# Two attention layers over eight images on one core: first query/key half moved to the last logits step, image 0's start reordered

## The chip, the cores and the metric

The kernel runs on one core of a Trainium2 chip. The metric is the device time of one launch in microseconds (us), lower is better. Five engines work side by side, each through its own instruction queue in order, and semaphores tie them together: TensorE (PE, matrix products into PSUM; PEld in the profile is its loading of weights), VectorE (DVE), ScalarE (ACT), GpSimd (POOL) and SyncE (SP, which here issues all transfers).

## The reference

For each of 8 images with 256 channels and 32x32 = 1024 pixels:

```python
# layer 0: self-attention with 32-channel query and key
q, k, v = Wq@x + bq, Wk@x + bk, Wv@x + bv          # 32, 32, 256 channels
x = gamma * (v @ softmax(q.T @ k).T) + x
# layer 1: group norm (32 groups), attention with 256-channel query and key
h = group_norm(x) * norm_w + norm_b
q, k, v = q_w@h + q_b, k_w@h + k_b, v_w@h + v_b
x = x + proj_w @ (v @ softmax(q.T @ k / 16).T) + proj_b
```

Everything is float32. The kernel splits a float32 operand into a rounded high part and a low remainder (`_hi`, `_lo`) and makes each product of three faster ones: high by high, high by low, low by high.

## The kernel before, in words

An image is 2 channel tiles of 128 by 1024 columns, in two halves of 512. Every 1024-column stage is cut into 8 tiles of 128 rows. Layer 0 of an image first makes `qk` (query and key projection, two entries, one for each half), `value0` (4 entries) and `scores` (8 tiles, only for the row maximum and the row sum of exponentials). From these comes a shift of each row, taken into the query operand by `shift`. `keys` (8 tiles) are the transposed scores with the shift, whose exponentials are the probabilities. `values(0, image, k)` multiplies value tile k by probability tile k and accumulates four PSUM banks over k (12 matmuls of 512 columns for each k). Layer 1 has `norm` (group sums), `query`, `value1`, `logits` (8 tiles, 12 matmuls each) and its own `values(1, ...)`.

PSUM is a `ring` of 4 slots of 1024 columns. Slots 2 and 3 hold the four accumulating banks of `values`; slots 0 and 1 pass all other results. An entry put into a slot waits until the reader of the entry before it there is done (`wait_read`, L583). A `scores` tile is read by DVE (row maximum, L1058) and then by ACT (exponential with row sum, L841); a `keys` tile by ACT (L817); a `qk` entry by ACT (L879, L884) and DVE (L1022, L1023, L1030). A probability tile goes through ACT (exponential, then the high part, L831 or L834) and DVE (the low part, L1075 or L1078), and only then may `values` use it.

The order is written out by hand as a list of `Step`s (L84 to L213). On TensorE (L777) a step fills its own `tile`, its `early` entries, the first `banks_first` banks of its `values`, its `sides`, the other banks, and its `late` entries. ACT and DVE walk over the same list in orders of their own (L906, L1135). `turn(i)` (L155) gives 16 steps: 0 to 7 make the keys of image i, 8 to 15 the logits of image i-1; `values` run two steps behind. In it `qk` of image i+1 has its first half late in step 0 and its second half in step 3, and `scores` of image i+1 begin in step 4. Image 1 has its turn written as `ones`; `turn` runs for images 2 to 7.

At the start (`first_image`, L84) TensorE is kept busy with products of ones (`keep_busy`, L590) while the first image is loaded in two halves of columns and split (L802, L955); then come `qk` and `value0` 0 and 1 of image 0, its 8 `scores` with `value0` 2 and 3 between them, `qk` of image 1, the shift (L635), and the keys steps. In the keys steps of image 0, step k+2 has `scores` k of image 1, always in slot 0.

Of the kernel before, what the change touches and what calls it, by code (L numbers as in the profile page):

```python
# [34 lines left out]
class Step:  # L35
# [6 lines left out]
    def __init__(self, tile=None, values=None, banks_first=2, slots=(0, 1)):  # L42
        self.tile, self.values, self.banks_first, self.slots = tile, values, banks_first, slots
        self.early, self.sides, self.late = [], [], []
        self.early_log = self.log = self.shifts = self.hidden = self.hidden_lo = self.split_x = self.x_lo_mid = self.x_lo_end = None
        self.statistics = self.evacuate = self.evacuate_at_once = None
        self.take_weights = self.keep_values = self.opening = self.rest = self.low_first = False
        self.early_in_front = False
        self.hidden_mid = None
# [34 lines left out]
def first_image():  # L84

    start, scores, opening = Step(slots=(0, 1, 2, 3)), Step(slots=(0, 1, 2)), Step()
    start.sides = tiles("qk", 0, (0, 1)) + tiles("value0", 0, (0, 1))
    scores.late = tiles("scores", 0, (0, 1, 2)) + tiles("value0", 0, (2,)) + tiles("scores", 0, (3, 4, 5))
    scores.late += tiles("value0", 0, (3,)) + tiles("scores", 0, (6, 7))
    scores.keep_values = True  # L90
# [7 lines left out]
    for k in range(6):  # L98
        steps[k + 2].early = tiles("scores", 1, (k,))
    steps[4].sides = tiles("value0", 1, (0,))  # L100
    steps[6].sides = tiles("value0", 1, (1,))
# [12 lines left out]
def second_image():  # L114
# [35 lines left out]
    ones[6].sides = tiles("shift", 2, (0,))  # L150
    ones[5].split_x, ones[5].x_lo_end, ones[6].x_lo_mid = 3, (3, 0), (3, 1)
    return steps + ones


def turn(i):  # L155
# [14 lines left out]
    if has(i + 1):  # L170
        steps[0].late = tiles("qk", i + 1, (0,))
        steps[3].banks_first = 0
# [21 lines left out]
    else:  # L194
# [3 lines left out]
        for m, s in enumerate((14, 15)):  # L198
            steps[s].late = tiles("query", i, (m,))
    if has(i + 2):  # L200
        steps[13].split_x, steps[13].x_lo_end, steps[14].x_lo_mid = i + 2, (i + 2, 0), (i + 2, 1)
    return steps
# [63 lines left out]
def values_done(tile):  # L266
# [12 lines left out]
    "v1_full", "v1_hi", "value1_split", "stats_ready", "norm_read", "coef_ready", "h_full", "h_hi", "h_split",  # L279
    "x_hi", "x_split", "res0_ready", "res1_ready", "weights_read", "weights_split", "rows_ready", "bias_read",  # L280
    "layer0_split", "v0_weights", "small_ready", "ones_ready", "key_hi", "link", "pool_link",
# [3 lines left out]
def build(nc, x, wqk_t, bqk, bk0, wv0_t, bv0, gamma, norm_w, norm_b, wq, bq, wk, bk, wv, bv, wp_t, bp,  # L285
          ident, group, y):
    with ExitStack() as ctx:
# [160 lines left out]
        def _(pool):  # L448
# [8 lines left out]
            def first_split_x():  # L457
                pool.wait_ge(x_loaded[1], x_loads(1))
                hi, lo = x_split(1)
                for half in range(HALVES):  # L460
                    cols = half_cols[half]
                    G.tensor_copy(hi[:, :, cols], x_in[1][:, :, cols]).then_inc(S["x_hi"], 1)
                    pool.wait_ge(S["x_hi"], 2 + half + 1)
                    G.tensor_tensor(lo[:, :, cols], x_in[1][:, :, cols], hi[:, :, cols].bitcast(F32),
# [112 lines left out]
        def _(pe):  # L577
# [139 lines left out]
            def fill(entry):  # L717
# [25 lines left out]
                else:  # L743
                    last = bias_products(SLOT[entry])
                last.then_inc(S["ring_ready"], 1)

            def values(tile, banks):
# [27 lines left out]
            wait("ones_ready", 1)  # L775
            keep_busy(ring[:, 3], 30)
            for now in STEPS:  # L777
                front = [now.tile] * bool(now.tile)
                for entry in now.early + front if now.early_in_front else front + now.early:
                    fill(entry)  # L780
                if now.values:
                    values(now.values, range(now.banks_first))
                for entry in now.sides:
                    fill(entry)
# [6 lines left out]
        def _(act):  # L791
# [3 lines left out]
            def split_x(i):  # L795
                for half in range(HALVES):
# [3 lines left out]
                    else:  # L800
                        act.wait_ge(x_loaded[i % 2], x_loads(i))
                    copy(x_hi[:, :, cols], x_in[i % 2][:, :, cols]).then_inc(S["x_hi"], 1)  # L802

# [49 lines left out]
            def project_hi(entry):  # L853
# [9 lines left out]
                if kind == "value0":  # L863
# [4 lines left out]
                    elif i:  # L868
                        copy(v0_hi[:, 2 * m:2 * m + 2], got).then_inc(S["value0_hi"], 1)
                if kind == "qk":  # L870
                    query_part(entry)
                    key_part(entry)

            def query_part(entry):
                _, i, m = entry
                if i == 0 and m == 0:
                    act.wait_ge(S["bqk_loaded"], 16 * 2)
                act.wait_ge(S["ring_ready"], RING_NO[entry] + 1)
                activation(q4[i % 2][0:64, half_cols[m]], half_place(entry)[0:64], ACT.Identity,  # L879
                           bias=bqk_s[0:64]).then_inc(S["qk_hi"], 1)  # L880

            def key_part(entry):
# [54 lines left out]
        def _(dve):  # L937
# [12 lines left out]
            scale = C ** -0.5  # L950

            def split_x(i, half):
                cols = half_cols[half]
                dve.wait_ge(S["x_hi"], 2 * i + half + 1)
                V.tensor_tensor(x_lo[:, :, cols], x_in[i % 2][:, :, cols], x_hi[:, :, cols].bitcast(F32),  # L955
# [10 lines left out]
            def first_weights():  # L966
                dve.wait_ge(S["wqk_loaded"], 16)
                split(wqk_hi[:], wqk_lo[:], wqk_f).then_inc(S["layer0_split"], 1)
                for half in range(HALVES):
                    split_x(0, half)  # L970

# [44 lines left out]
            def key_part(entry):  # L1016
# [4 lines left out]
                k, cols, out = k4[i % 2], half_cols[m], half_place(entry)  # L1021
                link(V.tensor_scalar(k[0:32, cols], out[64:96], bqk_s[64:96], None, ALU.add))  # L1022
                V.scalar_tensor_tensor(k[32:64, cols], out[64:96], bk0_s[:], k[0:32, cols].bitcast(F32),  # L1023
# [111 lines left out]
            for now in STEPS:  # L1135
# [28 lines left out]
                for entry in first:  # L1164
                    if entry[0] != "norm":
                        follow(entry)
# [9 lines left out]
                for entry in first:  # L1176
                    if entry[0] == "norm":
                        follow(entry)
# [48 lines left out]
```

## Time and profile before

| | |
|---|---|
| median of 3 runs | 795.13 us (795.07 to 798.98) |
| profiled execution | 795.73 us, its span 793.9 us |
| TensorE busy | 780.9 us, 98% |
| VectorE busy | 550.3 us, 69% |
| ScalarE busy | 468.8 us, 59% |
| GpSimd busy | 165.8 us, 21% |

The span is the time from the first to the last recorded instruction; the execution's own time is a little longer. Busy time is the sum of an engine's instructions, and says nothing yet of who waited for whom. "idle before, releaser" in a row of instructions is how long the engine stood idle in front of it and whose end let it go.

### The profile page before, as it was taken

To read this page: it belongs to the slowest core of one execution; us is meant where nothing else is said; L and a number is where in the kernel's file an instruction comes from. 1 tells how busy PE (TensorE), PEld (TensorE's weight loads), DVE (VectorE), ACT (ScalarE), POOL (GpSimd) and SP (SyncE) were. 2 spreads that over 40 slices of the span, in tenths; PEclk is the share of its full clock that TensorE was granted. 3 is DMA by queue.
4 is the path that set the end of the run, shared out by engine and by line. 5 is a ranking of instruction groups with operands and counts; after the bars stand their busy time and mean duration, and the time that the engine had idled before them with its cause. 6 is when DMAs were issued, how large, how long until landed. Compare 5 with 4: busy or idle time off the path is not lost.

```text
span 793.9 us, 9812 instructions
## 1 busy us (share of the span) xinstructions
PE 780.9 (98%) x3816; PEld 645.5 (81%) x3816; DVE 550.3 (69%) x790; ACT 468.8 (59%) x603; POOL 165.8 (21%) x147
## 2 busy tenths in 40 slices
PE   9899999999999999999999999999999999999998
PEld 8677888887888878887788877888778888888886
DVE  5866867777578765787657885577856756486564
ACT  4876656667555764567655586456864556445343
POOL 5640052013100231004210141102310024101120
PEclk9999999999999999999999999999999999999999
DMA  6010010002000110001100011000100001000101
GB/s 186 0 54 1 1 53 1 1 16 92 1 1 1 54 53 1 1 1 53 54 1 1 1 53 54 2 0 1 54 1 1 0 1 54 1 0 1 54 1 53
DMA packets 10366, 18.98 MB, mean 24 GB/s; under 512 B 2129, under 2 KB 3921, under 8 KB 10321
## 3 DMA queue, kind: packets, MB, share of 16 engines
q1 hardware_dynamic: 10320, 18.36, 6.7%
q8 instruction: 30, 0.49, 0.3%
q14 instruction: 16, 0.12, 0.1%
HBM read 9.97 MB, written 8.39 MB: 23 GB/s over the span
## 4 chain that ended last, share of the span: by engine, by line
PE 85%; DVE 9%; ACT 4%; issue 1%; POOL 0%; ACTq 0%; DVEq 0%; POOLq 0%
PE ring L596 26%; PE ring L598 25%; PE ring L597 25%; PE ring L606 4%; PE ring L616 3%; DVE res L1111 2%; DVE pt_lo L1075 2%; DVE h_lo L963 1%; ACT ring L841 1%; DVE q L1030 1%; PE ring L593 1%; DVE k L1022 1%; ACT pt_hi L831 1%; DVE k L1023 1%; ACT prob L817 1%
## 5 line engine op out<-in xcount | busy, mean ns | idle before, releaser
L596 PE MATMUL ring<-pt_hi,v_hi 128*128 128x512 f32 x480 | 189.1, 394 | 0.1
L598 PE MATMUL ring<-pt_hi,v_lo 128*128 128x512 f32 x480 | 187.9, 391 | 0.0
L597 PE MATMUL ring<-pt_lo,v_hi 128*128 128x512 f32 x480 | 187.7, 391 | 0.0
L820 ACT ACTIVATE prob<-ring,neg_max 128x1024 f32<-128x1024 f32 x64 | 71.6, 1119 | 156.6 <-DVE neg_max L1061 156.6
L1060 DVE TENSOR_REDUCE neg_raw<-ring 128x1 f32<-128x1024 f32 x64 | 78.2, 1223 | 59.0 <-PE ring L598 58.9
L503 POOL TENSOR_TENSOR v_lo<-v_f,v_hi 128x512 fp32r<-128x512 f32 x28 | 37.8, 1349 | 384.6 <-ACT v_hi L858 384.6
L598 PEld LDWEIGHTS ring<-pt_hi,v_lo 128*128 128x128 f32 x480 | 90.1, 188 | 19.8
L596 PEld LDWEIGHTS ring<-pt_hi,v_hi 128*128 128x128 f32 x480 | 90.2, 188 | 19.1 <-issue 1.7
L597 PEld LDWEIGHTS ring<-pt_lo,v_hi 128*128 128x128 f32 x480 | 90.3, 188 | 17.6
L1058 DVE TENSOR_REDUCE neg_max<-ring 128x1 f32<-128x1024 f32 x64 | 77.7, 1222 | 37.4 <-PE ring L606 37.3
L1075 DVE TENSOR_TENSOR pt_lo<-prob,pt_hi 128x1024 fp32r<-128x1024 f32 x64 | 81.6, 1276 | 30.4 <-ACT pt_hi L831 30.2
L841 ACT ACTIVATE ring<-ring,neg_max 128x1024 f32<-128x1024 f32 x64 | 69.6, 1087 | 43.4 <-DVE neg_max L1058 43.2
L1078 DVE SCALAR_TENSOR_TENSOR pt_lo<-prob,row_inv,pt_hi 128x1024 fp32r<-128x1024 f32 x64 | 83.1, 1298 | 15.0 <-ACT pt_hi L834 15.0
L596 PE MATMUL ring<-h_hi,query_hi 128*128 128x512 f32 x224 | 88.1, 393 | 0.2 <-DVE query_lo L1005 0.2
L598 PE MATMUL ring<-h_hi,query_lo 128*128 128x512 f32 x224 | 87.5, 391 | 0.0
L597 PE MATMUL ring<-h_lo,query_hi 128*128 128x512 f32 x224 | 87.5, 391 | 0.0
L817 ACT ACTIVATE prob<-ring 128x1024 f32<-128x1024 f32 x64 | 65.4, 1022 | 35.4 <-PE ring L616 35.1
L834 ACT ACTIVATE pt_hi<-prob,row_inv 128x1024 fp32r<-128x1024 f32 x64 | 73.9, 1154 | 11.0 <-DVE row_inv L1067 10.8
L831 ACT CAST pt_hi<-prob 128x1024 fp32r<-128x1024 f32 x64 | 67.4, 1054 | 5.3
L596 PEld LDWEIGHTS ring<-h_hi,query_hi 128*128 128x128 f32 x224 | 42.1, 188 | 9.3 <-DVE query_lo L1005 0.4
L598 PEld LDWEIGHTS ring<-h_hi,query_lo 128*128 128x128 f32 x224 | 42.0, 188 | 9.0
L597 PEld LDWEIGHTS ring<-h_lo,query_hi 128*128 128x128 f32 x224 | 42.1, 188 | 8.6
(167 smaller groups left out, 1347.1 us busy)
## 6 DMA issues: line engine op xcount, KB each, us to landing
out_y<-res SPq DMA_DIRECT2D x32, 256.0 KB, 2.2
x_in<-in_x SPq DMA_DIRECT2D x7, 1024.0 KB, 4.9
x_in<-in_x SPq DMA_DIRECT2D x2, 512.0 KB, 5.7
h_f<-in_wv_t SPq DMA_DIRECT2D x1, 256.0 KB, 4.0
res<-in_wq SPq DMA_DIRECT2D x1, 256.0 KB, 6.9
res<-in_wk SPq DMA_DIRECT2D x1, 256.0 KB, 7.2
res<-in_wv SPq DMA_DIRECT2D x1, 256.0 KB, 7.7
res<-in_wp_t SPq DMA_DIRECT2D x1, 256.0 KB, 7.4
```

The costliest lines, as they stand in the source:

```text
L596: mm(out, w_hi, m_hi, start=first, stop=False)
L597: mm(out, w_hi, m_lo, start=False, stop=False)
L598: return mm(out, w_lo, m_hi, start=False, stop=last)
L817: activation(prob[:, p % PROBS], ring[:, slot], ACT.Exp).then_inc(S["keys_exp"], 1)
L820: activation(prob[:, p % PROBS], ring[:, slot], ACT.Exp, bias=neg_max[:, k % 2:k % 2 + 1], accum_out=row_sum[:, k % 2:k % 2 + 1]).then_inc ...
L831: copy(pt_hi[p % PT][:], prob[:, p % PROBS]).then_inc(S["p_hi"], 1)
L834: activation(pt_hi[p % PT][:], prob[:, p % PROBS], ACT.Identity, scale=row_inv[:, k % 2:k % 2 + 1]).then_inc(S["p_hi"], 1)
L841: activation(ring[:, slot], ring[:, slot], ACT.Exp, bias=neg_max0[:, k:k + 1], accum_out=row_sum0[:, k:k + 1]).then_inc(S["scores_exp"], 1)
L1058: V.tensor_reduce(neg_max0[:, k:k + 1], src, AX_X, ALU.max, negate=True).then_inc(S["scores_max"], 1)
L1060: link(V.tensor_reduce(neg_raw[:, k % 2:k % 2 + 1], src, AX_X, ALU.max, negate=True))
L1075: V.tensor_tensor(lo[:], src, hi[:].bitcast(F32), ALU.subtract).then_inc(S["p_split"], 1)
L1078: V.scalar_tensor_tensor(lo[:], src, row_inv[:, k % 2:k % 2 + 1], hi[:].bitcast(F32), ALU.mult, ALU.subtract).then_inc(S["p_split"], 1)
```

## The change

Six edits:

1. `turn(i)` loses `qk` (i+1, half 0) from the end of step 0 and gets `qk` (i+2, half 0) in the sides of step 15, the last logits step; image 3's goes to the last step of `ones`. On DVE the entry is followed after the row inverse (and an evacuation, if the step has one) instead of ahead of them.
2. In image 0, `value0` 3 goes behind all eight `scores`; behind each of `scores` 3 to 6 come two passes of products of ones into the place that `value0` 3 will take. The warm-up has 28 passes instead of 30.
3. In keys steps 2 and 3 of image 0 (`scores` 0 and 1 of image 1) all four banks of `values` come first, and the `scores` tile behind them.
4. Image 0's x is split in quarters (one channel tile of one half) in place of halves, on ACT and on DVE, with a semaphore of its own.
5. Of the second `qk` half of image 0, the first key part is written by ACT, not by DVE.
6. The counts of `x_hi` are renumbered for it.

```diff
-    scores.late = tiles("scores", 0, (0, 1, 2)) + tiles("value0", 0, (2,)) + tiles("scores", 0, (3, 4, 5))
-    scores.late += tiles("value0", 0, (3,)) + tiles("scores", 0, (6, 7))
+    scores.late = tiles("scores", 0, (0, 1, 2)) + tiles("value0", 0, (2,)) + tiles("scores", 0, (3, 4, 5, 6, 7))
+    scores.late += tiles("value0", 0, (3,))
...
+    for s in (2, 3):
+        steps[s].banks_first, steps[s].early_behind = BANKS, True
...
+    ones[7].sides = tiles("qk", 3, (0,))
...
     if has(i + 1):
-        steps[0].late = tiles("qk", i + 1, (0,))
...
     if has(i + 2):
+        steps[15].sides = tiles("qk", i + 2, (0,))
...
+                if kind == "scores" and i == 0 and 3 <= m < TILES - 1:
+                    keep_busy(half_place(("value0", 0, 3)), 2)
...
-            keep_busy(ring[:, 3], 30)
+            keep_busy(ring[:, 3], 28)
             for now in STEPS:
                 front = [now.tile] * bool(now.tile)
                 for entry in now.early + front if now.early_in_front else front + now.early:
-                    fill(entry)
+                    if not (now.early_behind and entry in now.early):
+                        fill(entry)
                 if now.values:
                     values(now.values, range(now.banks_first))
+                if now.early_behind:
+                    for entry in now.early:
+                        fill(entry)
...
+                    if i == 0:
+                        for ct in range(CT):
+                            copy(x_hi[:, ct, cols], x_in[0][:, ct, cols]).then_inc(S["x0_hi"], 1)
+                    else:
+                        copy(x_hi[:, :, cols], x_in[i % 2][:, :, cols]).then_inc(S["x_hi"], 1)
...
+                    if (i, m) == (0, 1):
+                        first_key_part(entry)
                     query_part(entry)
                     key_part(entry)
...
+            def first_key_part(entry):
+                act.wait_ge(S["ring_ready"], RING_NO[entry] + 1)
+                activation(k4[0][0:32, half_cols[entry[2]]], half_place(entry)[64:96], ACT.Identity,
+                           bias=bqk_s[64:96]).then_inc(S["key_first"], 1)
...
+            def first_split_x(half):
+                cols = half_cols[half]
+                for ct in range(CT):
+                    dve.wait_ge(S["x0_hi"], CT * half + ct + 1)
+                    last = V.tensor_tensor(x_lo[:, ct, cols], x_in[0][:, ct, cols], x_hi[:, ct, cols].bitcast(F32),
+                                           ALU.subtract)
+                last.then_inc(S["x_split"], 1)
...
-                link(V.tensor_scalar(k[0:32, cols], out[64:96], bqk_s[64:96], None, ALU.add))
+                if (i, m) == (0, 1):
+                    dve.wait_ge(S["key_first"], 1)
+                else:
+                    link(V.tensor_scalar(k[0:32, cols], out[64:96], bqk_s[64:96], None, ALU.add))
...
                 for entry in first:
-                    if entry[0] != "norm":
+                    if entry[0] != "norm" and not logits:
                         follow(entry)
                 if logits:
                     row_inverse(now.tile)
                     pending = now.tile
...
                 for entry in first:
-                    if entry[0] == "norm":
+                    if entry[0] == "norm" or logits:
                         follow(entry)
```

## Rows read from the trace of the kernel before

**Rows 1.** The page: busy time by engine, share of the span, instructions.

```profile
PE 780.9 (98%) x3816; PEld 645.5 (81%) x3816; DVE 550.3 (69%) x790; ACT 468.8 (59%) x603; POOL 165.8 (21%) x147
```

**Rows 2.** The waits of TensorE: us in total, times, longest.

```profile
PE ring L606 <- DVE q L1030: 3.4, 6, 0.7
PE ring L606 <- ACT ring L841: 2.7, 5, 1.5
PE ring L635 <- DVE shift_pair L1085: 1.4, 1, 1.4
PE ring L606 <- ACT prob L817: 0.4, 1, 0.4
```

**Rows 3.** A middle stretch: length, busy us of PE, PEld, DVE, ACT, POOL; TensorE's clock; DMA; GB/s.

```profile
285.00:380.00 95.00, 94.52 (x462) 77.79 (x461) 67.58 (x99) 57.96 (x77) 17.05 (x15) 1.00 0.06 23
```

**Rows 4.** The warm-up's products of ones (L593) alone, in two stretches.

```profile
0.00:5.00 5.00, 4.03 (x19) 4.03 (x20) 1.00 0.55 130
5.00:9.60 4.60, 4.60 (x43) 4.60 (x42) 1.00 0.93 266
```

**Rows 5.** Instructions in order of time (start, duration), from image 0's projections to its first scores.

```profile
10.76 1.29 POOL L512 TENSOR_TENSOR wv_lo<-h_f,wv_hi 128x512 fp32r<-128x512 f32 x1
...
12.46 0.28 PE L596 MATMUL ring<-wv_hi,x_hi 128*128 128x256 f32 x1
...
13.46 0.69 ACT L884 ACTIVATE k<-ring,bqk_s 32x512 fp32r<-32x512 f32 x1
...
15.20 0.74 DVE L1030 SCALAR_TENSOR_TENSOR q<-ring,bqk_s,q 32x512 fp32r<-32x512 f32 x1
...
16.20 1.63 PE L606 MATMUL ring<-k,q 96*128 96x512 f32 x6 [0.74 <-DVE q L1030]
```

**Rows 6.** Image 0's scores to its shift: one stretch, then instructions by engine.

```profile
22.00:23.00 1.00, 1.00 (x5) 0.86 (x5) 0.97 (x2) 1.00 (x3) 0.92 (x2) 0.52 0.00 0
...
16.94 7.01 DVE L1058 TENSOR_REDUCE neg_max<-ring 128x1 f32<-128x1024 f32 x6 [1.00 <-PE ring L606]
...
27.21 1.09 ACT L841 ACTIVATE ring<-ring,neg_max 128x1024 f32<-128x1024 f32 x1 [2.03 <-DVE neg_max L1058]
...
30.51 0.64 PE L635 MATMUL ring<-ident_r,shift_pair 128*2 128x128 f32 x8 [1.38 <-DVE shift_pair L1085]
...
31.19 1.00 ACT L851 CAST q<-ring 2x1024 fp32r<-2x1024 f32 x1 [0.29 <-PE ring L635]
```

**Rows 7.** Keys steps 1 to 4 of image 0: low parts, exponential, the two scores tiles.

```profile
35.22 1.22 DVE L1075 TENSOR_TENSOR pt_lo<-prob,pt_hi 128x1024 fp32r<-128x1024 f32 x1 [0.34 <-ACT pt_hi L831]
...
38.06 1.91 DVE L1075 TENSOR_TENSOR pt_lo<-prob,pt_hi 128x1024 fp32r<-128x1024 f32 x1 [0.42 <-ACT pt_hi L831]
...
42.39 0.73 PE L606 MATMUL ring<-k,q 96*128 96x512 f32 x2 [1.46 <-ACT ring L841]
...
44.42 1.09 ACT L841 ACTIVATE ring<-ring,neg_max 128x1024 f32<-128x1024 f32 x1
...
46.15 0.63 PE L606 MATMUL ring<-k,q 96*128 96x512 f32 x2
```

**Rows 8.** Last logits step of one turn to step 4 of the next (image 3's keys).

```profile
263.94 1.12 ACT L820 ACTIVATE prob<-ring,neg_max 128x1024 f32<-128x1024 f32 x1 [2.85 <-DVE neg_max L1061]
...
266.63 1.28 DVE L1078 SCALAR_TENSOR_TENSOR pt_lo<-prob,row_inv,pt_hi 128x1024 fp32r<-128x1024 f32 x1 [1.28 <-ACT pt_hi L834]
...
269.92 0.40 PE L596 MATMUL ring<-pt_hi,v_hi 128*128 128x512 f32 x1
...
272.26 2.48 DVE L1111 TENSOR_TENSOR res<-ring,res 128x512 f32<-128x512 f32 x4
...
280.75 0.63 PE L616 MATMUL ring<-q,k 98*128 98x512 f32 x2
...
280.86 0.74 DVE L1030 SCALAR_TENSOR_TENSOR q<-ring,bqk_s,q 32x512 fp32r<-32x512 f32 x1
...
281.86 0.70 PE L606 MATMUL ring<-k,q 96*128 96x512 f32 x2 [0.48 <-DVE q L1030]
```

More of the change, by code:

```diff
@@ L47, in __init__ @@
         self.take_weights = self.keep_values = self.opening = self.rest = self.low_first = False
-        self.early_in_front = False
+        self.early_in_front = self.early_behind = False
         self.hidden_mid = None
@@ L279 @@
     "v1_full", "v1_hi", "value1_split", "stats_ready", "norm_read", "coef_ready", "h_full", "h_hi", "h_split",
-    "x_hi", "x_split", "res0_ready", "res1_ready", "weights_read", "weights_split", "rows_ready", "bias_read",
+    "x0_hi", "x_hi", "x_split", "key_first", "res0_ready", "res1_ready", "weights_read", "weights_split", "rows_ready", "bias_read",
     "layer0_split", "v0_weights", "small_ready", "ones_ready", "key_hi", "link", "pool_link",
@@ L462, in first_split_x @@
                     G.tensor_copy(hi[:, :, cols], x_in[1][:, :, cols]).then_inc(S["x_hi"], 1)
-                    pool.wait_ge(S["x_hi"], 2 + half + 1)
+                    pool.wait_ge(S["x_hi"], half + 1)
                     G.tensor_tensor(lo[:, :, cols], x_in[1][:, :, cols], hi[:, :, cols].bitcast(F32),
@@ L801, in split_x @@
                         act.wait_ge(x_loaded[i % 2], x_loads(i))
-                    copy(x_hi[:, :, cols], x_in[i % 2][:, :, cols]).then_inc(S["x_hi"], 1)
+                    if i == 0:
[3 more added lines that the diff above has]
+                        copy(x_hi[:, :, cols], x_in[i % 2][:, :, cols]).then_inc(S["x_hi"], 1)
             def hidden(i):
@@ L950, in _ @@
             scale = C ** -0.5
+            def first_split_x(half):
[5 more added lines that the diff above has]
+                last.then_inc(S["x_split"], 1)
             def split_x(i, half):
                 cols = half_cols[half]
-                dve.wait_ge(S["x_hi"], 2 * i + half + 1)
+                dve.wait_ge(S["x_hi"], 2 * (i - 1) + half + 1)
                 V.tensor_tensor(x_lo[:, :, cols], x_in[i % 2][:, :, cols], x_hi[:, :, cols].bitcast(F32),
@@ L969, in first_weights @@
                 for half in range(HALVES):
-                    split_x(0, half)
+                    first_split_x(half)
             def biases(slot):
```

## The prediction

> **What bounds the kernel now.** I read the busy shares first: TensorE is busy for 98% of the span, 780.9 of 793.9 us [rows 1]. The table of stretches says where the missing 13 us lie: a middle stretch of 95 us is idle for only 0.5 us [rows 3]; the rest is the start, and the end behind the last product, which no edit touches. So only three things can gain: work taken off TensorE, a lower clock avoided, or a wait removed. The waits of TensorE [rows 2] name the last: 3.4 us in 6 waits for DVE's query part, 2.7 in 5 for ACT's exponential of a scores tile, 1.4 for the shift. TensorE's work is unchanged but for products of ones, so all comes from waits and the clock.
>
> **Edit 2a, the warm-up.** The rows of L593 show 19 products in the first 5 us and 43 in the next 4.6 [rows 4]: 0.107 us each once it is fast, two to a pass, so 0.21 a pass. Two passes less are -0.43 us, not a fifteenth of 8.6 us. The first projection moves from 9.59 to 9.16. That it may start then needs x's low part by then; the half that took 1.05 us on ACT from 6.53 and about 1.3 on DVE is there by 8.9, in quarters, overlapped (edit 4), by about 8.5. Edit 4 thus gains nothing by itself before the second half (9.9 instead of 10.2, wanted at 10.6): 0.
>
> **Edit 5 and the first scores.** Before, DVE ran six parts of 0.75 us in series, the last (L1030) ended at 15.94, and the scores began 0.26 later, at 16.20 [rows 5]. Now ACT writes one of the six. ACT's queue from 10.90: query 0.70, key 0.70, first key part 0.70 to 13.0, query to 13.7, key to 14.4 (an ACT part is 0.69 us) [rows 5]. DVE: three parts from 10.91 to 13.19, then 13.22 to 13.97 and 13.99 to 14.73; scores may begin at 14.99. Behind ACT's extra part stands `value0` 0's copy, late by 0.3 us and wanted only at 16.1. But the products of `value0` stand in front of the scores: they began at 12.46 and would now be due at 12.03, where POOL's low part of the weights ends only at 12.05 [rows 5], plus 0.25 for the signal: 12.3. From there 24 products of 0.118 us end at 15.13. So the scores begin at 15.13: **-1.07**.
>
> **Edit 2b, the row of scores.** DVE's maxima come every 1.17 us (7.01 for six), and then DVE and ACT stood still for 2.0 us [rows 6], because `scores` 6 was behind `value0` 3 on TensorE, whose clock was down (0.52 in 22.00 to 23.00, mostly the 1.2 GHz level). With `value0` 3 last, `scores` 6 is filled when `scores` 3 has been read, in time for the seventh maximum; maxima and exponentials run through. From 15.13: the eight maxima end at 25.23, the last exponential at 26.43, the shift pair is ready 0.99 later, at 27.42 (that took the same 0.99 before). TensorE: `scores` 7 at 22.94, `value0` 3 to 24.82, `qk` of image 1 (12 products of 0.235) to 27.64. It now comes last, so L635 starts at 27.64 instead of 30.51 [rows 6]: -2.87. The eight passes of ones (8 x 0.21 us) lie in gaps: a tile comes each 1.13 us and takes 0.47 + 0.43, so they cost nothing while the clock is up; without that cover they would cost 1.7. ACT's copy of the shift before was at 31.19; now it waits for ACT's query part of `qk` 1, to 28.55, and keys begin at 29.75 in place of 32.34. So 0.27 of the 2.87 go: start to first keys **-2.6**, the -1.07 among it.
>
> **Edit 3, the moved scores tiles.** TensorE waited 0.43 us in front of `scores` 0 of image 1 [rows 2] and 1.46 in front of `scores` 1 [rows 7]. Both go, but I see the wait come back one tile later. In the times of before: `values` 0 can start at 36.65, when the low part that ended at 36.44 is signalled [rows 7], and runs 2.73 us; `scores` 0 at 39.38, keys 0.47, `values` 1 at 40.32 (its low part ends at 39.97), `scores` 1 at 43.05, keys at 43.52. At 43.99 TensorE wants `scores` 2, which the change leaves in front of its `values`, in slot 0, where `scores` 1 must first be read: product to maximum to exponential took 3.24 us from the start of the product at 42.39 to the end of the exponential and its sum (44.42 + 1.21) [rows 7]. So it starts at 43.05 + 3.3 = 46.35, where before it started at 46.15 without a wait [rows 7]: **+0.2**. The bounds: -1.9, if both waits just went, and +0.6, if ACT, which now has an exponential and a high part of keys ahead of that of `scores` 1, is the later one. I take the value of the chain, as its two rows are of this place.
>
> **Edit 1, the turns.** Each of five turns has one wait left: keys at 280.75, then `scores` at 281.86, where two products of keys take 0.47 [rows 8]. The spacing lost is 0.64 us, of which the idle column shows 0.48; the first of the five lost 0.85. DVE had no gap from 269.9 to that point: `qk`'s first half (three parts, 2.25 us), then the evacuation at 272.26, low parts, the second half, whose end at 281.60 releases TensorE. Moved into step 15, the first half's three parts run from 265.35 to 267.64, where DVE had stood idle for 1.28 us [rows 8]. Then: low part of the last logits tile 267.75 to 269.03, of keys 0 to 271.1, the evacuation from 271.15, held by its fourth bank (its products end at 272.9) to 273.6 instead of 274.5. The hidden low parts follow ACT's high parts and end at 277.25, and the query part ends at 280.8 instead of 281.6. TensorE wants it at 281.22 with 0.25 of signal: 0.17 us of margin. So the whole spacing goes: 0.85 + 4 x 0.64 = **-3.4**. The evacuation that starts earlier also takes away 0.2 us that the first bank of `values` (0, 2, 0) stood late in the first turn: **-0.2**.
>
> What is queued behind the moved entry: on TensorE six products (1.41 us) go ahead of two banks and of keys 0, no more work in all. Keys 0 now takes the slot of logits 7, whose exponential ends at 265.15 [rows 8] and which is wanted at 266.24: 1.1 us of cover. On ACT two parts (1.37 us) stand in front of the high part, which ends at 267.7 instead of 266.6, and the low part, at 269.03 instead of 267.91, is wanted by `values` at 269.92 [rows 8]: 0.9 us of cover. No transfer is moved: SP's and POOL's queues keep their order, only stores start about 1 us earlier.
>
> **The sum**: -2.6 + 0.2 - 3.4 - 0.2 = -6.0. Against the profiled execution, 795.73 us (span 793.9 and 1.8 around it), that is 789.7; that execution was 0.6 above the median of 795.13, from which it is 789.1. I say **789.4**, -0.7%.
>
> **The rivals.**
> A: *the clock falls all the same* in the row of scores, or in the new pause of 2.3 us before `scores` 2. For it: it fell behind four short waits for ACT (1.2 us together, the 2.7 of five without the longest [rows 2]), and with 0.90 of 1.13 us filled the gaps are smaller, not gone. Against it: 1.38 and 1.46 us of pause (L635 and `scores` 1) did not lower it. The stretch at the low level lasted some 3.4 us (22.1 to 25.4 by windows of 0.25); in the row of scores that makes a tile 1.8 us instead of 1.13 for two tiles, +1.3, in the pause up to +1.9. Sum -4.7 to -4.1: 791.1. The Trainium skill, "TensorE: Matmul & The Clock Gate", section "A second HAM failure mode: psum-queue depth-cycling", says that frequent short idles between groups of matmuls can make the clock swing between its levels. By that rule the trace agrees in its fall at 22.0, and the remaining gaps of 0.2 us speak for this rival.
> B: *the wait of the turns changes its name*. The margin of 0.17 us is the thinnest here, and DVE or ACT (high parts of keys and hidden ahead of the second query part) may be later than reckoned. If all of it stays: -2.6, 792.8.
> C: *the pause before `scores` 2 does not come*, if the exponential is read sooner: -1.9 for +0.2, 787.3.
> D, *slower*: ACT's two and DVE's three parts stand in front of the probabilities of logits 7. If they run in series and not side by side (ACT's high part at 267.7, DVE's parts behind, 2.25, then 1.28), the low part ends at 271.2, and `values` stand 1.3 to 1.5 us in each of five turns: 7.4 - 2.4 = +5, 800.4. It decides from a low part that ends 0.5 us behind 269.9; DVE's parts wait for nothing of ACT's high part, which speaks against it.
>
> **Chances.** Forecast 0.52, A 0.20, B 0.13, C 0.10, D 0.05. What a measurement of this kernel can tell from no change is 0.5%, 4.0 us: faster begins below 791.15. The forecast and C are faster nearly whole, A in half, B not: faster 0.70, same 0.25, slower 0.05. The range holds C at its low end and nearly B at its high: 787.0 to 792.4; the likeliest case alone is 788.6 to 790.4.
>
> **What would show it.** First scores at 15.1; L635 at 27.6; TensorE's clock 1.00 from 15 to 30; a new wait of some 2.3 us in front of `scores` 2 of image 1 for ACT L841, none in front of 0 and 1; the row of waits for DVE q gone or under 0.5 us; middle stretches of 95 us idle below 0.1. It is wrong if `scores` 2 starts at once, if L1078 of logits 7 ends after `values` want it, or if turns do not lose 0.6 us each.

## The result, and the profile after

Changed kernel: median **792.3 us** (790.98 to 796.32, 17 runs); kernel before, beside it: 796.8 us (794.94 to 800.13, 17 runs). Ratio 0.9946 [0.9932, 0.9960], that is -4.3 us [-5.4, -3.2]. Forecast: 789.4, by a sum of -6.0 us. The profiled execution took 793.57 us, span 791.8. Two of the twelve executions of c2_start_only below, of 1173 and 1988 us, were slow ones and are left out of every figure.

The page of the changed kernel, busy time by engine and the chain by engine; they answer to [rows 1].

```profile
PE 782.5 (99%) x3828; PEld 648.5 (82%) x3828; DVE 553.9 (70%) x791; ACT 468.8 (59%) x606; POOL 160.8 (20%) x147
...
PE 95%; DVE 2%; ACT 2%; issue 1%; POOL 0%; ACTq 0%; DVEq 0%; POOLq 0%
```

TensorE is busy 1.6 us longer than in [rows 1]: it has 12 more instructions (16 for the passes of ones in the row of scores, less 4 of the warm-up), and its stretch at the lower clock, 3.4 us long in both traces, lies at 77 us, where TensorE is full, and no longer at 22 us among waits. Its waits, against [rows 2] (us in total, times, longest):

```profile
PE ring L609 <- ACT ring L854: 2.4, 3, 2.0
PE ring L596 <- POOL unit L546: 1.0, 1, 1.0
PE ring L599 <- DVE v_lo L1039: 0.9, 1, 0.9
PE ring L599 <- issue: 0.7, 1, 0.7
PE ring L619 <- ACT q L864: 0.5, 1, 0.5
```

DVE's query part (3.4 us in [rows 2]) and the shift (1.4) are gone; one wait of 2.0 for the exponential is there, where 1.5 stood before; and two are new, 0.7 in front of `values` 0 (given as `issue`) and 0.9 for `v_lo`.

Stretches of the changed kernel (length, busy us and instructions of PE, PEld, DVE, ACT, POOL; TensorE's clock; DMA; GB/s): the middle, the row of scores, and one of 2 us at 78. The first answers to [rows 3], the second to the stretch in [rows 6].

```profile
285.00:380.00 95.00, 94.98 (x464) 78.45 (x464) 68.64 (x98) 58.80 (x76) 16.98 (x14) 1.00 0.06 23
20.00:30.00 10.00, 9.48 (x57) 7.68 (x56) 9.47 (x13) 9.14 (x17) 5.48 (x8) 1.00 0.00 0
78.00:80.00 2.00, 2.00 (x11) 2.00 (x10) 2.00 (x3) 0.66 (x1) 0.00 (x0) 0.50 0.00 0
```

Middle idle 0.02 us, was 0.48. Clock 1.00 all through the scores row, was 0.52 at 22. But at 78 it is 0.50, the 1.2 GHz level.

The start: GpSimd's low part of the weights, the first products of `value0`, DVE's last query part, the scores, the shift, its copy, the first keys.

```profile
10.30 1.29 POOL L515 TENSOR_TENSOR wv_lo<-h_f,wv_hi 128x512 fp32r<-128x512 f32 x1
...
12.31 0.28 PE L599 MATMUL ring<-wv_hi,x_hi 128*128 128x256 f32 x1
...
14.27 0.74 DVE L1062 SCALAR_TENSOR_TENSOR q<-ring,bqk_s,q 32x512 fp32r<-32x512 f32 x1
...
15.27 1.62 PE L609 MATMUL ring<-k,q 96*128 96x512 f32 x6
...
27.79 0.64 PE L638 MATMUL ring<-ident_r,shift_pair 128*2 128x128 f32 x8
...
28.69 1.00 ACT L864 CAST q<-ring 2x1024 fp32r<-2x1024 f32 x1
...
29.84 1.16 PE L619 MATMUL ring<-q,k 98*128 98x512 f32 x4 [0.50 <-ACT q L864]
```

Keys steps 1 to 3 of image 0, by engine; they answer to [rows 7].

```profile
32.30 1.27 POOL L528 TENSOR_TENSOR v_lo<-x,v_hi 128x512 fp32r<-128x512 f32 x1
...
32.71 1.94 DVE L1107 TENSOR_TENSOR pt_lo<-prob,pt_hi 128x1024 fp32r<-128x1024 f32 x1 [0.90 <-ACT pt_hi L844]
...
34.75 0.47 PE L599 MATMUL ring<-pt_hi,v_hi 128*128 128x512 f32 x1 [0.69 <-issue]
...
41.25 0.63 PE L609 MATMUL ring<-k,q 96*128 96x512 f32 x2
...
43.17 1.09 ACT L854 ACTIVATE ring<-ring,neg_max 128x1024 f32<-128x1024 f32 x1 [0.47 <-DVE neg_max L1090]
...
44.43 0.73 PE L609 MATMUL ring<-k,q 96*128 96x512 f32 x2 [2.02 <-ACT ring L854]
```

A turn, against [rows 8]: the moved first half's first part, the low part of logits 7, the evacuation, the last query part, and `scores`, which no longer waits.

```profile
265.37 0.74 DVE L1054 TENSOR_SCALAR k<-ring,bqk_s 32x512 fp32r<-32x512 f32 x1
...
267.68 1.28 DVE L1110 SCALAR_TENSOR_TENSOR pt_lo<-prob,row_inv,pt_hi 128x1024 fp32r<-128x1024 f32 x1
...
270.99 2.62 DVE L1143 TENSOR_TENSOR res<-ring,res 128x512 f32<-128x512 f32 x4
...
279.75 0.74 DVE L1062 SCALAR_TENSOR_TENSOR q<-ring,bqk_s,q 32x512 fp32r<-32x512 f32 x1
...
281.04 0.63 PE L609 MATMUL ring<-k,q 96*128 96x512 f32 x2
```

**Where the time went, by landmarks.** Each image's first shift product (L635 before, L638 after, other line numbers in the experiments) is in every trace. From their starts: a = start of the first; b = first to second (edit 3 is here); c = second to third; d = third to the last (five turns).

| kernel | a | b | c | d |
|---|---|---|---|---|
| before | 30.51 | 40.56 | 90.20 | 478.54 |
| changed | 27.79 | 41.42 | 92.90 | 475.51 |
| changed, run again (b1) | 27.72 | 41.38 | 91.73 | 475.55 |
| edit 1 alone (c1) | 30.71 | 40.56 | 94.41 | 475.29 |
| changed without edit 1 (c2) | 27.97 | 41.35 | 90.12 | 478.61 |
| edit 3 undone (b2) | 28.09 | 40.62 | 90.12 | 475.57 |
| one scores tile behind one bank (c3) | 27.30 | 39.61 | 93.32 | 475.44 |
| changed with passes of ones at the bias products (f1) | 27.34 | 42.83 | 91.47 | 475.50 |
| the same, edit 3 undone (f2) | 28.06 | 40.50 | 91.48 | 475.51 |
| c3 with passes at the bias products (d3) | 28.18 | 39.65 | 91.49 | 475.55 |
| d3 with d4's wait (f3) | 27.96 | 39.47 | 91.45 | 475.51 |

Before to changed: -2.72, +0.86, +2.70, -3.03, together -2.2, as the spans (793.9 to 791.8). The profiled execution of before has no loss in c and that of the changed kernel has one, so the two traces show less than the medians (-4.3).

### The profile page after: what moved, and what is told of

Read it like the earlier page. It is cut to its first block, busy times and chain, and to the rows that moved or that the text cites. A ratio compares the mean times of both kernels' runs of the same rounds, so it can differ in the third digit from the quotient of the medians.

```text
span 791.8 us, 9841 instructions
## 1 busy us (share of the span) xinstructions
PE 782.5 (99%) x3828; PEld 648.5 (82%) x3828; DVE 553.9 (70%) x791; ACT 468.8 (59%) x606; POOL 160.8 (20%) x147
## 4 chain that ended last, share of the span: by engine, by line
PE 95%; DVE 2%; ACT 2%; issue 1%; POOL 0%; ACTq 0%; DVEq 0%; POOLq 0%
PE ring L599 29%; PE ring L601 28%; PE ring L600 28%; PE ring L609 4%; PE ring L619 4%; PE ring L596 1%; ACT ring L854 1%; DVE neg_max L1090 0%; PE ring L638 0%; ACT pt_hi L844 0%; ACT prob L830 0%; DVE x L1140 0%; DVE res L1143 0%; DVE h_lo L992 0%; PE ring L701 0%
## 5 line engine op out<-in xcount | busy, mean ns | idle before, releaser
L1107 DVE TENSOR_TENSOR pt_lo<-prob,pt_hi 128x1024 fp32r<-128x1024 f32 x64 | 84.9, 1327 | 33.8 <-ACT pt_hi L844 33.5
```

The costliest lines, as they stand in the source:

```text
L1107: V.tensor_tensor(lo[:], src, hi[:].bitcast(F32), ALU.subtract).then_inc(S["p_split"], 1)
```

## The experiments

Ratios are to the kernel before, run on the same chip, with 95% intervals. The groups b and f ran on one chip, c on a second, d on a third, so times of different groups are compared by their ratios alone.

**b1_changed.** No edit.

> The changed kernel once more, as the measure for the others of this group. Theory 1 (the start and the turns gain as forecast, and a lower clock that comes in some executions and contention between DVE and POOL take some back): -3.8 to -4.6 us against before; its profile again has the wait of 2.0 us before scores 2 of image 1, middle stretches idle below 0.1 us in 95, and, if the clock falls, falls at another place than 77 to 81 us. Theory 2 (the change itself makes the clock fall behind the bias products of image 1): the fall is at 77 to 81 us again, costs 1.7 us, every time.

0.9943 [0.9926, 0.9960], median 792.2. The result stands. The clock fell again at 77 to 81 us; the wait for `v_lo` did not come.

**b2_no_behind.** Edit 3 undone, all else kept.

```diff
-    for s in (2, 3):
-        steps[s].banks_first, steps[s].early_behind = BANKS, True
```

> The changed kernel with scores 0 and 1 of image 1 in front of values 0 and 1 again, as before (edit 3 undone). Theory 1 (the wait only moves one tile on, and the reorder costs a little): the two waits of 0.4 and 1.5 us for ACT's exponential are back, that of 2.0 us before scores 2 is gone, and the time is equal to the changed kernel's within 0.5 us, by my chain 0.2 to 0.8 us faster. Rival (the reorder gains what its two waits cost): 1.5 to 1.9 us slower than the changed kernel.

0.9922 [0.9898, 0.9945], median 790.7: 1.7 us better than b1, though the intervals overlap, and more than the 0.2 to 0.8 expected. Its wait for the exponential, against 2.4 (longest 2.0) in the changed kernel:

```profile
PE ring L607 <- ACT ring L852: 1.3, 3, 0.9
```

**b3_no_fill.** Without the eight passes of ones in the scores row.

```diff
-                if kind == "scores" and i == 0 and 3 <= m < TILES - 1:
-                    keep_busy(half_place(("value0", 0, 3)), 2)
```

> The changed kernel without the eight passes of ones behind scores 3 to 6 of image 0. Theory 1 (they keep the clock up in the row of scores): the profile shows the 1.2 GHz level for some 3.4 us between 20 and 26 us, value0 3 and the scores run at half speed there, and the time is 1.0 to 1.5 us more than the changed kernel's. Rival (they are idle weight; the fall of the clock came from the pause before the first scores, which is gone anyway): no fall there, same time within 0.3 us.

0.9962 [0.9946, 0.9979], median 794.1: by the two ratios the passes are worth 1.5 us. Its stretches in the scores row:

```profile
22.00:24.00 2.00, 1.75 (x5) 1.01 (x5) 1.89 (x2) 2.00 (x5) 1.92 (x3) 0.56 0.00 0
24.00:28.00 4.00, 4.00 (x17) 3.71 (x16) 2.52 (x3) 2.54 (x5) 0.49 (x1) 0.50 0.00 0
```

The clock is at its lower level again from 22 us on, here for 6.8 us (22.2 to 29.1), twice as long as in the kernel before (22.0 to 25.5). All twelve executions have a mean clock of 0.991 to 0.996, where the kernel before reaches 0.999 and 1.000 in four of 21 beside them. So the reorder alone does not keep the clock up, the passes do.

**b4_spread.** Scores 2, 3 and 4 go behind 3, 1 and 1 banks of their step's value products as well.

```diff
-    for s in (2, 3):
-        steps[s].banks_first, steps[s].early_behind = BANKS, True
+    for s, first in ((2, BANKS), (3, BANKS), (4, 3), (5, 1), (6, 1)):
+        steps[s].banks_first, steps[s].early_behind = first, True
```

> The changed kernel with scores 2, 3 and 4 of image 1 put behind three, one and one banks of their step's values too, so that the distance between two scores tiles never falls under some 3 us of TensorE's work. Theory 1 (the moved wait is a chain of product, maximum and exponential, 3.3 us long, with only 0.5 us of work beneath it): the wait of 2.0 us before scores 2 shrinks to three of at most 0.3 us, and the time is 1.4 to 1.8 us less than the changed kernel's. Rival (DVE or ACT is the bound of this stretch, whatever the order): the wait goes to another instruction, the same time within 0.4 us.

0.9929 [0.9909, 0.9949], median 791.5. The 2.0 us before `scores` 2 went (0.4 in 2 is left), and this stood in its place:

```profile
PE ring L619 <- DVE v_lo L1039: 1.2, 1, 1.2
```

Part b is 41.19, hardly below 41.4: a pause filled in one place came back at the keys.

**c1_turns_only** and **c2_start_only.** Edit 1 alone on the kernel before, and the changed kernel without it (the cut shows edit 1's lines in the list of steps; c1 also has its two lines on DVE, which c2 keeps).

```diff
+    ones[7].sides = tiles("qk", 3, (0,))
-        steps[0].late = tiles("qk", i + 1, (0,))
+        steps[15].sides = tiles("qk", i + 2, (0,))
```

> The kernel before with edit 1 alone (first query/key half in the last logits step). Theory 1 (it takes away the wait of every turn, and nothing else): -2.8 to -3.6 us against before, 0.34 to 0.84 us in each of five turns; the waits for DVE's query part shrink from 3.4 us in 6 to 0.7 in 1; the clock still falls at 22 us. Rival B (the wait changes its name): less than -1.0 us.

> The changed kernel with edit 1 undone (all edits of the start alone). Theory 1 (the start gains 2.7 us up to image 0's shift, and 1 to 2 of them are lost again behind it): -1.0 to -2.0 us against before, 2.8 to 3.4 more than the changed kernel; waits for DVE's query part 2.7 us in 5. Theory 2 (the start keeps what it gains to the first keys): -2.5 us or more.

c1: 0.9965 [0.9950, 0.9981], -2.8 us [-4.0, -1.5]. c2: 0.9987 [0.9973, 1.0001], -1.0 us [-2.1, +0.1]. Together -3.8, and both at once -4.3 to -4.5: within their intervals they add up. In c2's waits the query part of the turns is still there:

```profile
PE ring L608 <- DVE q L1061: 2.6, 5, 0.7
PE ring L608 <- ACT ring L853: 2.4, 3, 2.0
```

**c3_one_behind.** `scores` 0 of image 1 in front again, `scores` 1 behind one bank instead of all four.

```diff
-    for s in (2, 3):
-        steps[s].banks_first, steps[s].early_behind = BANKS, True
+    steps[3].banks_first, steps[3].early_behind = 1, True
```

> The changed kernel with scores 0 of image 1 in front of its values again, and scores 1 behind one bank of them instead of four. Theory 1 (the chain of product, maximum and exponential wants a distance of 3.3 us to either side, so a tile is best put in the middle): waits for ACT's exponential of together about 0.5 us in this stretch, 1.3 to 2.0 us less than the changed kernel, as the one with edit 3 undone or up to 0.4 us less. Rival (any place costs the same, what was gained there was the clock alone): the time of the changed kernel.

0.9927 [0.9902, 0.9951], median 791.7, in two groups: 788.2 and 788.4 at mean clock 0.999, 791.6 to 793.0 at 0.995 and 0.996. Part b is the shortest of all, 39.61. Its waits:

```profile
PE ring L608 <- ACT ring L853: 0.7, 3, 0.2
PE ring L608 <- ACT prob L829: 0.4, 1, 0.4
```

**c4_bias_fill.** Four passes of ones at the head of the bias entry. Behind them come its two products of 256 columns and then the 12 of one column (24 instructions in the trace, 73.1 to 75.8 us in the changed kernel, where the clock fell at 77; the expectation's "20 products of 1 or 2 columns" is wrong).

```diff
                 else:
+                    keep_busy(ring[:, SLOT[entry], HALF:], 4)
                     last = bias_products(SLOT[entry])
```

> The changed kernel with four passes of ones (0.85 us) ahead of the bias products of image 1's first steps, 20 products of 1 or 2 columns each, behind which its clock fell at 77 us in two profiles. Theory 2 (the fall follows from that sparse stretch, and a filler ahead of it helps): no fall at 77, and the median is 0 to 0.9 us less than the changed kernel's. Rival (the fall comes with the place in the chip's own beat, whatever stands there): falls in as many executions, mean clocks from 0.993 to 1.000 as before, and the time 0.85 us more.

0.9961 [0.9946, 0.9977], median 793.4: the clock fell all the same, at 76.8 to 80.3, 0.3 us behind the last narrow product, and the passes cost their time on top.

**d1_pool_later.** GpSimd's first residual waits for DVE's hidden low parts.

```diff
             def residual1(i):
+                if i == 0:
+                    pool.wait_ge(S["h_split"], CT)
```

> The changed kernel, with POOL's first residual of layer 1 (image 0, around 101 to 105 us) held until DVE has written both hidden low parts. Theory (in some executions POOL's instruction starts just ahead of DVE's low part of 103 us, which then takes 2.2 instead of 1.25 us, and the query products start 0.9 us late): no execution has this wait, the profile's low part there takes 1.2 to 1.3 us, and the median is 0.2 to 0.6 us less than the changed kernel's. Rival (the late residual only moves the collision to the evacuation at 115 us): a new wait of up to 1 us, time equal or more.

0.9947 [0.9935, 0.9959]. The wait of 0.9 for `v_lo` did not come, but it had not come in b1 either, and the ratio is the same: nothing shown.

**d2_half_dense.** It leaves out six of the 12 narrow bias products (each sum is its first product alone) and has six passes of ones between the others.

```diff
                 for j in range(2):
-                    for o in range(CT):
-                        mm(value_b_ps[:, C + j:C + j + 1], bq_rows[:, o], bk_s[:, o:o + 1], ...
+                    mm(value_b_ps[:, C + j:C + j + 1], bq_rows[:, 0], bk_s[:, 0:1], start=True, stop=True)
+                    keep_busy(ring[:, slot, HALF:], 1)
```

> The changed kernel with half of the 12 narrow bias products (1 column) left out and six passes of ones between the others, so that the stretch takes the same time but has no long row of narrow products (the biases are then half of theirs). Theory (the clock falls at 77 us because of this row): mean clock 0.999 or 1.000 in nearly all executions, no fall at 77, median 0.5 to 1.2 us less than the changed kernel's. Rival (the fall comes with the chip's own beat): clocks from 0.993 to 1.000 as before, same time.

0.9946 [0.9934, 0.9958], median 791.4. Its stretch at 78, to be set beside that of the changed kernel:

```profile
78.00:80.00 2.00, 2.00 (x16) 1.89 (x15) 2.00 (x3) 1.42 (x2) 0.00 (x0) 1.00 0.00 0
```

No fall in this profile; mean clocks 0.997 to 1.000 and the times close together (791.1 to 791.9). On this chip that says little by itself: the changed kernel with d1's wait, without passes, had none either (0.998 to 1.000).

**d3_best_dense.** c3 with all bias products kept and a pass of ones ahead of each of the six groups.

```diff
                 for j in range(2):
+                    keep_busy(ring[:, slot, HALF:], 1)
                     for o in range(CT):
...
                     for out, w, b in ((rowk_ps, wq_f, bk_s), (query_b_ps, wk_f, bq_s)):
+                        keep_busy(ring[:, slot, HALF:], 1)
                         for o in range(CT):
```

> The changed kernel with scores 1 of image 1 behind one bank (scores 0 in front), and six passes of ones between all bias products, which add 1.3 us of TensorE's time. Theory (narrow row lowers the clock): 0.999 or 1.000 in nearly all executions, all of them near 788.2 + 1.3 = 789.5 us, ratio 0.991 to 0.992. Rival: some of the executions at 0.996 and 793 us, median 792 or more.

0.9934 [0.9922, 0.9946], median 790.7, 790.1 to 790.9, all clocks 0.999 or 1.000. Part c is 91.49 where it is 90.12 with neither fall nor passes (b2): the six passes cost 1.3 us, 6 x 0.21, in every execution, and save 3.2 (93.32 in c3) where a fall of 6.8 us would have come.

**d4_pool_start.** GpSimd's last low part of image 0's values waits for DVE's second low part of keys.

```diff
-            for m in (2, 3):
-                first_values0(m)
+            first_values0(2)
+            pool.wait_ge(S["p_split"], 2)
+            first_values0(3)
```

> The changed kernel with POOL's split of value0 3 (image 0) held until DVE has written the first two low parts. Theory (the first low part takes 1.94 us instead of 1.22, because POOL had started 0.4 us ahead of it, and all behind it is 0.65 us late): the first low part takes 1.2 us, values 0 start 0.5 to 0.7 us earlier after keys 0, scores 2 too, and the time is 0.5 to 1.0 us less. Rival (the wait before scores 2 absorbs it, or POOL's work comes late for the next loads): no gain.

0.9954 [0.9937, 0.9970]. DVE's low part, alone now, against 1.94 us in the changed kernel:

```profile
32.42 1.23 DVE L1108 TENSOR_TENSOR pt_lo<-prob,pt_hi 128x1024 fp32r<-128x1024 f32 x1 [0.97 <-ACT pt_hi L845]
```

Part b fell from 41.4 to 40.71, so 0.7 us is there in the trace; the ratio does not show it (two of its seven executions took 794.0 and 795.0 us at a mean clock of 0.996).

**f1_changed_dense, f2_no_behind_dense, f3_best_pool, f4_before_dense.** The passes of d3 in four kernels: the changed one; it with edit 3 undone; c3 with d4's wait; the one before.

> The changed kernel with six passes of ones between the narrow bias products (+1.3 us of TensorE's time). Theory 1 (the narrow row lowers the clock in half of the executions, 1.7 us each time): mean clocks 0.999 to 1.000, median 791.5 to 792.5 us, so about the changed kernel's own, with less spread. Rival (no link): clocks down to 0.994, median 793.5.

> The same with edit 3 undone. Theory 1 (edit 3 costs 0.5 to 1.0 us by itself: one chain wait of 2.0 us and 0.65 us of a slowed low part against waits of 0.4 and 0.9): 0.4 to 1.0 us less than the changed one of this group. Rival (what edit 3 cost was the clock): the same within 0.3 us.

> Scores 0 of image 1 in front, scores 1 behind one bank, the passes between the bias products, and POOL's split of value0 3 held until two low parts are written. If both gains add (2.3 us of the place of the scores, 0.6 us of the low part): 2.5 to 3 us less than the changed one of this group, 789 us; if POOL's delay only matters where values stand behind the first low part: 1.5 to 2.2 us less.

> The kernel before with the same passes. Theory 1 (its own median holds falls at 77 us too): the time of the kernel before plus 0 to 1.3 us; against it the changed one of this group is 4.0 to 5.0 us faster. Rival (the clock of the kernel before did not fall at 77, only that of the changed one does): plus 1.3 us, and the changed one of this group is 5.5 to 6.0 us faster.

f1 0.9964 [0.9952, 0.9977], median 793.2; f2 0.9945 [0.9932, 0.9959], 791.6; f3 0.9934 [0.9922, 0.9947], 790.6; f4 1.0004 [0.9991, 1.0017], 797.1. f1 against f2 repeats b1 against b2: edit 3 costs 1.5 us, and here all five executions with it (792.7 to 793.7) lie above all five without (790.1 to 792.6). And f1's profile shows what I had called rival A, behind the pause of 2.0 us before `scores` 2:

```profile
44.00:46.00 2.00, 2.00 (x8) 1.64 (x9) 1.31 (x2) 1.88 (x3) 2.00 (x3) 0.86 0.03 8
46.00:48.00 2.00, 2.00 (x10) 1.90 (x10) 1.25 (x1) 1.11 (x2) 1.91 (x2) 0.50 0.00 0
48.00:50.00 2.00, 2.00 (x11) 1.73 (x10) 0.40 (x1) 0.59 (x1) 1.92 (x3) 0.79 0.00 0
```

The clock is at the 1.2 GHz level from 45.4 to 48.8, and part b is 42.83. The same pause of 2.0 us did not lower it in the other eight profiles that have it (the changed kernel, b1, b3, c2, c4, d1, d2, d4). The mean clock was 0.998 in four of f1's five executions and 1.000 in four of f2's five.

f4 says that the passes alone bring the kernel before nothing, and more: f1 is 4.0 us below f4 (medians 793.15 and 797.11). With the passes in both, so that neither has the fall at 77 us in its profile, the change is worth no more than without them, so that fall does not account for what lacks to the forecast's 6.0 us. f2, without edit 3, is 5.5 us below f4.

f3 is 2.6 us below f1; but against d3, which lacks only the wait, its part b is just 0.2 shorter (39.47, 39.65): GpSimd's delay pays where `values` 0 stand right behind the first low part, and there `scores` 0 stands between them.

b2 (0.9922), c3 (0.9927), b4 (0.9929), d3 and f3 (0.9934) are the best versions with all of the work, ahead of the changed kernel by 1 to 2 us; their intervals overlap its own.

## Why the prediction was right and wrong

**Edit 2a, the warm-up: off.** The first projection starts at 9.42, 0.17 earlier and not 0.43. Four products of ones fewer run, but more of them at the first pace of 0.21 us: 21 here, 18 before, 16 to 24 over all traces, which puts the first projection of the kernels with 28 passes anywhere from 8.88 to 9.77. So a single trace can't show 0.43 us.

**Edit 5 and the first scores: the number right, in part by luck.** 15.27 against 15.13 forecast. But `value0` did not wait for GpSimd's low part of the weights, as I had reckoned: that ended at 11.59 and not 12.05, and the products of `value0` followed the projections without a gap at 12.31, 2.9 us behind the first projection, as in all 18 traces (2.88 to 2.89). The forecast's 12.3 came out because the projection was 0.26 late and the supposed wait had put 0.27 on top. What edit 5 itself gives is the distance from the first projection to the scores, 6.61 us before and 5.85 now: -0.76; the other 0.17 of the gain are the warm-up's.

**Edit 2b, row of scores: right.** Shift at 27.79 (27.64), copy at 28.69 (28.55), keys at 29.84 (29.75): -2.50 since before, forecast -2.6. The eight passes lie in gaps and keep the clock up; b3 prices them at 1.5 us. (Of the "four short waits" that rival A puts ahead of the old fall, three, 1.0 us, lie there; the fourth is at 64.46.)

**Edit 3, "+0.2": this is the step that failed.** The mechanism was as put: both old waits went, and the wait came back before `scores` 2 for the exponential, 2.02 us (2.3 forecast). Its size was wrong, in two parts. The first is steady: from the first keys to the second shift it is 38.73 us before (71.07 less 32.34) and 39.37 now (69.21 less 29.84), +0.64; and against the changed kernel without the edit (b2) part b is 0.8 longer. `values` 0 was reckoned from the low part of before, 1.22 us [rows 7]; here it took 1.94, because GpSimd's low part (L528) had begun 0.41 us ahead of it, at 32.30, where in [rows 7] DVE had begun, at 35.22, 0.16 us ahead of GpSimd's, and GpSimd's was the long one:

```profile
35.38 2.20 POOL L525 TENSOR_TENSOR v_lo<-x,v_hi 128x512 fp32r<-128x512 f32 x1
```

So `values` 0 started 4.91 us behind the first keys (34.75 less 29.84), where 4.31 was reckoned (36.65 less 32.34), and all behind it 0.6 later. That is the new wait of 0.7 in front of them. The low part is long in b2 as well (1.88), but there `scores` 0 stands ahead of `values` 0 and covers it. d4 takes it away: `values` 0 start 4.20 behind the first keys, and from these to the second shift it is 38.66 us, against 38.56 in b2, so there edit 3 costs 0.1 in the trace, close to the +0.2 forecast. The second part is the clock: in f1's profile the new pause is followed by some 3.4 us at the lower level, and b is 1.4 longer. I had given that a chance in rival A as a case of its own, and not as something that happens in a share of the executions. By the ratios the edit costs 1.7 us (b2 against b1) and 1.5 (f2 against f1) where +0.2 was forecast. Without it the kernel comes to 0.9922, -6.2 us [-8.1, -4.4], and the sum without its term was -6.2 too. Where I went wrong is the comparison: I set the new wait against the two that it replaced, and did not ask which engine would then be first beside DVE, nor what a place between (c3: part b 39.61, 1.8 us shorter) would give.

**Edit 1, -3.4 and -0.2: right in its mechanism, somewhat too large.** Alone, in c1, it takes 3.25 us off part d (475.29 against 478.54), all five turns among it: 0.86, 0.61, 0.60, 0.60 and 0.59; forecast were 0.85 and four times 0.64. c1's ratio gives -2.8. The 0.2 of the first bank did not show. Step by step: first part at 265.37 (265.35), low part of logits 7 from 267.68 to 268.96 (to 269.03), evacuation from 270.99 (271.15) to 273.6 (273.6), query part ending at 280.49 (280.8), `scores` without a wait.

In the changed kernel part d fell by 3.03 only, because one turn (351 to 447) is 0.3 longer than its neighbours. That is not edit 1: c1 does not have it, and c2, without edit 1, does (96.21 among 95.88 to 95.91), as have all kernels with the edits of the start. The place is the same each time, one exponential of a keys tile which ACT starts 0.3 us later behind its product, and the weight load that waits for it:

```profile
390.44 1.02 ACT L830 ACTIVATE prob<-ring 128x1024 f32<-128x1024 f32 x1 [1.74 <-PE ring L619]
...
391.52 0.19 PEld L599 LDWEIGHTS ring<-wpv_hi,h_hi 128*128 128x128 f32 x1 [0.43 <-ACT prob L830]
```

A turn earlier the two idle times are 1.46 and 0.17. Why ACT is late there is open.

**The sum.** The steady terms of the trace are -2.72 + 0.86 - 3.03 = -4.9 (the 0.86 holds 0.22 of edit 2b, forecast 0.27), within the interval of the ratio, -5.4 to -3.2. Of the 1.1 us that lack to -6.0, 0.4 are edit 3 against its +0.2, 0.6 the turns (0.2 the bank that did not show, 0.2 what d lacks to c1's, the rest spread over the turns), 0.1 the start. By the ratios 1.7 us lack, and of these edit 3 takes 1.3 to 1.5. How much of that is the clock the runs don't part; the one execution of f1 at a mean clock of 1.000 took 792.74, still above the four of f2 at 1.000 (790.09 to 792.59).

The Trainium skill, "TensorE: Matmul & The Clock Gate", section "A second HAM failure mode: psum-queue depth-cycling", says that short repeated idles between groups can swing the clock. b3 agrees: its fall comes in the row of short waits, at 22 us, and eight passes end it. The falls at 77 are not of that form: TensorE is busy 2.00 of 2.00 us in the stretch at 78, and what stands ahead are the narrow bias products.

**The second stretch, c: +2.70, in no step.** 0.92 of it is TensorE standing for `v_lo` at 109.62, because DVE's low part at 103.14 took 2.17 us beside GpSimd's residual, which had begun at 103.02; it is in this execution and in c1's, not in b1's. The rest is the fall at 77. c is 92.90 and 91.73 in two profiles of the same kernel, 90.20 in that of before, and c1, which is the kernel before with edit 1, has the fall too. It comes in some executions and not in others, so it explains why the two traces differ by 2.2 us only, and it does not account for the forecast's error: with passes there in both kernels the change is still -4.0 us (f1 against f4). Whether the edits make it more frequent is open.

Rivals: B did not come (no query wait); C did not (the pause is there); D did not (the low part of logits 7 ends 0.9 us before it is wanted). A came in part.

**Open:** why ACT is 0.3 us late in the one turn; what decides in which execution the clock falls; and how large the clock's share of edit 3's cost is: a fall behind the pause of 2.0 us was seen in one of the nine profiles that have the pause (f1).

## What to carry to other kernels

A tile whose slot is freed by a chain (product to maximum to exponential, 3.3 us here) needs that much TensorE work between it and the next tile of its slot. Moving it behind all the work of its step removes its own wait and makes the next tile's (2.0 us here); put it in the middle (c3: at most 0.2), and reckon the next two tiles. A duration read where one engine ran alone or first doesn't hold where the order of starts turns round: whenever a step moves by 2 us, see which instruction of the other engine now begins ahead of it. And passes of ones pay in a sparse row that otherwise lowers the clock each time, as in b3 (1.5 us gained in gaps that cost nothing); on a full TensorE they cost their whole length (d3: 1.3 us for six).

## What the runs showed of the hardware

**The one that starts first keeps its pace.** DVE's and GpSimd's subtractions, both from SBUF: DVE first by 0.16 us, at 35.22, took 1.22 us [rows 7] and GpSimd 2.20. GpSimd first by 0.41, at 32.30, took 1.27 and DVE 1.94. At 103 us in the changed kernel, GpSimd's residual (L491) first by 0.12, at 103.02, took 1.21 and DVE 2.17:

```profile
103.14 2.17 DVE L1107 TENSOR_TENSOR pt_lo<-prob,pt_hi 128x1024 fp32r<-128x1024 f32 x1 [1.18 <-ACT pt_hi L844]
...
109.62 0.50 PE L599 MATMUL ring<-h_hi,wqq_hi 128*128 128x512 f32 x1 [0.92 <-DVE v_lo L1039]
```

With starts closer than that the profile's times don't tell who wins: in b1 the residual stands 0.08 us ahead (102.92 against 103.00), yet it took 2.24 and DVE 1.25.

**A clock that falls at narrow products.** In five of the twelve profiles of kernels without passes there (the changed one, b1, c1, c3, c4) the clock went to the 1.2 GHz level at the bias products of one column: in c1 and c3 while they ran, for 6.8 us, in the others 0.3 to 1.4 us behind the last, for 3.4 us, each time with TensorE busy. In c3 they run from 70.8 to 74.2, and the clock falls at 72.7:

```profile
72.00:74.00 2.00, 2.00 (x14) 2.00 (x14) 0.95 (x1) 1.66 (x2) 0.00 (x0) 0.68 0.00 0
```

In the six with passes of ones between them (d2, d3, f1 to f4) it never did. Profiles alone are few for this, and three of the five are from the chip of group c, on which nothing with passes ran. The mean clocks of one chip say more, though not where the falls lay (a stretch of 3.4 us takes 0.002 off the mean): in group f it is 0.996 or less in four of 15 executions of the kernel before, in none of the 11 of the same kernel with the passes (f4), and in none of the 15 of f1 to f3. Four passes ahead of the whole entry (c4) did not keep it up.
